# A graph-network kernel on one core: where two kinds of rounds put their type sums and their next first code sums

## The reference, cut to what matters

```python
h = relu(layernorm(x) @ node_proj_w.T + node_proj_b)
for l in range(2):
    trans = einsum('nh,tdh->tnd', h, edge_W[l])          # 8 matrices of 128 x 128
    agg = segment_sum(trans[edge_type, src], dst, 6250)  # 100,000 edges
    h = relu(gru_cell(agg, h, ...))                      # gates r, z, n
return x + h @ out_w.T + out_b
```

## Time and profile before

| What | us |
|---|---|
| Median of 3 runs | 2007.2 |
| Lowest and highest of the runs | 2001.24, 2015.2 |
| The profiled execution | 2021.61 |
| Its span in the profile | 2019.8 |
| Mean granted share of TensorE's clock | 0.886 |

### The profile page before, as it was taken

One profiled execution on the slowest core, in us unless ns is written; L12 is line 12 of the kernel. 1 busy time (PEld: TensorE's weight loads), 2 busy tenths in 40 slices (PEclk: granted clock), 3 DMA queues, 4 the chain that ended last, 5 costly groups with the idle time before them and its releaser, 6 DMA issues.

```text
span 2019.8 us, 32542 instructions
## 1 busy us (share of the span) xinstructions
PE 1548.0 (77%) x10440; PEld 1066.8 (53%) x10441; DVE 806.9 (40%) x3362; ACT 499.7 (25%) x959; POOL 1194.0 (59%) x1277
## 2 busy tenths in 40 slices
PE   6477888787878866877883888878787786687877
PEld 3244555454555544655662555545545454565665
DVE  6656262523433244454442223212433224444444
ACT  5233151513324112222220101110423411121222
POOL 6555666565666666666625666565565666666661
PEclk9688899998999978898885998899898997888889
DMA  8323728264462422222213866674334255222221
GB/s 196 110 63 103 238 84 270 59 218 128 148 205 64 137 73 79 78 79 77 77 36 105 273 226 225 219 254 129 85 105 117 77 140 116 73 73 72 70 75 30
DMA packets 183275, 251.81 MB, mean 125 GB/s; under 512 B 24322, under 2 KB 156580, under 8 KB 183140
## 3 DMA queue, kind: packets, MB, share of 16 engines
q0 software_dynamic: 58176, 119.22, 21.7%
q1 hardware_dynamic: 118644, 128.45, 20.3%
q10 hardware_dynamic: 6320, 2.41, 0.5%
HBM read 211.87 MB, written 38.12 MB: 124 GB/s over the span
## 4 chain that ended last, share of the span: by engine, by line
PE 35%; another core or an unknown queue 31%; issue 11%; DVE 11%; DMA 4%; ACT 3%; DVEq 3%; SPq 2%; ACTq 0%; PEldq 0%
PE ps L1185 10%; PE ps L1257 5%; PE ps L1122 5%; PE ps L1162 4%; PE ps L1236 4%; DMA blocks<-node_table 4%; PE ps L1249 3%; PE ps L1228 2%; DVE acc L1850 1%; DVE onehot L1772 1%; DVE acc L1870 1%; ACT counts L871 1%; DVE onehot L1807 1%; DVE work L1728 1%
## 5 line engine op out<-in xcount | busy, mean ns | idle before, releaser
L660 POOL DMA_INDIRECT gath<-node_table,srcT x1212 | 1159.5, 957 | 774.7 <-issue 303.2
L1185 PE MATMUL ps<-counts,blocks 128*128 128x504 f16 (+3 forms) x1764 | 421.1, 386 | 66.8 <-issue 33.4
L1870 DVE TENSOR_TENSOR acc<-ps,acc 128x16 f32 x864 | 150.7, 174 | 792.4 <-remote 311.8
L950 ACT COPY sums_sb<-ps 128x512 f32<-128x512 f32 x216 | 126.3, 587 | 870.3 <-remote 600.3
L1185 PEld LDWEIGHTS ps<-counts,blocks 128*128 128x128 bf16 x1764 | 171.5, 101 | 266.1 <-issue 81.2
L1162 PE MATMUL ps<-work 128*128 128x392 bf16 x983 | 219.3, 358 | 119.5 <-ACT counts L871 43.2
L1257 PE MATMUL ps<-sums_sb,wT 128*128 128x128 f32 x1728 | 243.6, 299 | 59.9 <-ACT sums_sb L950 46.6
L1257 PEld LDWEIGHTS ps<-sums_sb,wT 128*128 128x128 f32 x1728 | 230.6, 212 | 74.6 <-ACT sums_sb L950 51.4
L1249 PE MATMUL ps<-onehot,gath 128*128 128x128 bf16 x2592 | 200.5, 230 | 62.6 <-issue 36.2
L1249 PEld LDWEIGHTS ps<-onehot,gath 128*128 128x128 bf16 x2592 | 177.8, 104 | 108.9 <-issue 74.9
L871 ACT CAST counts<-ps 128x392 f16<-128x392 f32 x429 | 188.3, 498 | 117.8 <-PE ps L1162 70.2
(11 more groups left out here) (209 smaller groups left out, 831.6 us busy)
## 6 DMA issues: line engine op xcount, KB each, us to landing
blocks<-node_table SPq DMA_DIRECT2D x84, 672.0 KB
kept_counts<-counts SPq DMA_DIRECT2D x28, 882.0 KB
counts<-kept_counts SPq DMA_DIRECT2D x28, 882.0 KB
gath<-node_table,srcT POOLq DMA_INDIRECT x1212
node_table<-gath SPq DMA_DIRECT2D x12, 360.0 KB, 4.5
node_table<-work SPq DMA_DIRECT2D x12, 360.0 KB
counts<-in_x_dram SPq DMA_DIRECT2D x1, 2880.0 KB
out_dram<-counts SPq DMA_DIRECT2D x12, 240.0 KB
```

What stands on the lines that cost most here:

```text
L660: nc.gpsimd.indirect_dma_start(out=gath[:, b, j, :], out_offset=None, in_=tables[l], in_offset=bass.IndirectOffsetOnAxis(ap=index, axis=0) ...
L950: act.copy(n_sb[:, b // 2, b % 2 * BG:(b % 2 + 1) * BG, :], narrow_sums[b % 2]) \
L1185: last = nc.tensor.matmul(head_ps[:, 0:COLS[share]], blocks[:, j % 2, at, part * H:(part + 1) * H], counts[:, a, 0:COLS[share]], start=(i ...
L1870: nc.vector.tensor_tensor(win, narrow_ps[q][:, g * NARROW:(g + 1) * NARROW], win, ALU.add) \
```

## The change

**Narrow rounds, PE.** The first types move behind sums 3. With a head the order becomes sums 0, head, sums 1, head, sums 2, head, sums 3, first types, head, second types. Without a head: sums 0, sums 1, r and hn, sums 2, in, sums 3, first types, z, second types, turning.

**Narrow rounds, DVE.** The one-hots of a half come ahead of everything else in it and wait for `sums_ready` of their slot instead of following the adds. The hots of the head come next, all of them ahead of the adds (`FIRST_HOTS` is gone).

**Narrow rounds, ACT, without head.** After copy 2 only tanh; the sigmoid of z comes after copy 3, with the new state and its rows.

**Late rounds, PE.** Sums 0 of the next round run between types 2 and types 3 of this one. The first late round's sums 0 run ahead of the loop, and the last round begins with its sums 1.

```diff
-                        update(b, n, begin, tile, head)
+                        if head is not None:
+                            head_slot(l, head + b)
+                        elif b == 1:
+                            piece(act, begin, gate_r, l + 1, tile)
+                        elif b == 2:
+                            piece(act, begin, gate_n, l + 1, tile)
+                        elif b == 3:
+                            piece(act, begin, gate_z_state, l + 1, tile)
+                def gate_z_state(s, i):
+                    gate_z(s, i)
+                    state_rows(s, i)
...
                     narrow_sums_of(k, 2)
                     if head is None:
                         piece(pe, begin, gate_in, l + 1, tile)
+                    else:
+                        head_slot(l, head + 2)
+                    narrow_sums_of(k, 3)
                     narrow_types(k, 0)
                     if head is None:
                         piece(pe, begin, gate_z, l + 1, tile)
                     else:
-                        head_slot(l, head + 2)
-                    narrow_sums_of(k, 3)
-                    if head is not None:
                         head_slot(l, head + 3)
                     narrow_types(k, 1)
...
                 def one_round(k, n, places):
                     begin, tile = round_tile(pe, mybir.EngineType.PE, n)
-                    sum_by_code(k, places[0][0], 0, places[0][1])
                     sum_by_code(k, places[1][0], 1, places[1][1])
...
                     by_type(k, 2)
+                    sum_by_code(k + SLOTS, places[SLOTS][0], 0, places[SLOTS][1])
                     by_type(k, 3)
                     piece(pe, begin, to_rows, l + 1, tile)
...
                 def last_round(k, places, begin=None):
-                    sum_by_code(k, places[0][0], 0, places[0][1])
...
-                def add_narrow(k, g0, q, after_head, hots):
-                    if len(hots) <= FIRST_HOTS:
-                        for g in hots:
-                            make_hots(g)
-                        hots = []
+                def add_narrow(k, g0, q, after_head):
...
-                            for more in hots[g * len(hots) // (2 * BG):(g + 1) * len(hots) // (2 * BG)]:
-                                make_hots(more)
...
                     for q in range(2):
                         g0 = n * ROUND + 2 * q * BG
+                        for b in (2 * q, 2 * q + 1):
+                            dve.wait_ge(sem_l["sums_ready"], k + (b + 1 + SLOTS))
+                            (one_hots if last else narrow_hots)(n * ROUND + (ROUND + b * BG), b)
                         if head is None and q == 0:
                             piece(dve, begin, before_tanh, l + 1, tile)
-                        hots = MADE[l].get(head + 2 * q, []) if head is not None else []
-                        add_narrow(k, g0, q, added_until(l, head + 2 * q) if head is not None else 0, hots)
-                        for b in (2 * q, 2 * q + 1):
-                            (one_hots if last else narrow_hots)(n * ROUND + (ROUND + b * BG), b)
+                        for g in MADE[l].get(head + 2 * q, []) if head is not None else []:
+                            make_hots(g)
+                        add_narrow(k, g0, q, added_until(l, head + 2 * q) if head is not None else 0)
```

More of the change, by code:

```diff
@@ L951, in narrow_round, with update @@
                            .then_inc(es[l]["sums_copied"], 1)
-                        update(b, n, begin, tile, head)
-                def update(b, n, begin, tile, head=None):
-                    if head is not None:
-                        head_slot(l, head + b)
-                    elif b == 1:
+                        if head is not None:
[9 more added lines that the diff above has]
+                    state_rows(s, i)
+                def update(b, n, begin, tile):
+                    if b == 1:
                         piece(act, begin, gate_r, l + 1, tile)
@@ L1296, in first_places @@
                 def first_places(phase, turns=0):
-                    places = [(phase + b) % PLACES for b in range(SLOTS)]
+                    places = [(phase + b) % PLACES for b in range(SLOTS + 1)]
                     return [(turns + ((phase + b) // PLACES + 1) * (16 * BG), place) for b, place in enumerate(places)]
                 def later_places(n):
-                    return [(n * (16 * BG) + 16 * BG, b) for b in range(SLOTS)]
+                    return [((n + b // SLOTS) * (16 * BG) + 16 * BG, b % SLOTS) for b in range(SLOTS + 1)]
                 def one_round(k, n, places):
                     begin, tile = round_tile(pe, mybir.EngineType.PE, n)
-                    sum_by_code(k, places[0][0], 0, places[0][1])
                     sum_by_code(k, places[1][0], 1, places[1][1])
@@ L1389, in _ @@
                 begun = NARROW_END * SLOTS - HEAD_BATCHES[l]
+                landed, place = first_places(begun)[0]
+                sum_by_code(NARROW_END * SLOTS, landed, 0, place)
                 with pe.Fori(0, turns) as t:
@@ L1406, in _ @@
                         pe.sem_inc(pass_begun, 1)
+                        sum_by_code(p * BATCHES, 16 * BG, 0, 0)
                         with pe.Fori(0, ROUNDS - 1) as n:
```

1 line of the change is left out of this document (removed).

## The result

| | us |
|---|---|
| median of before, beside the change (4 runs, 2001.2 to 2016.8) | 2011.2 |
| median of after (4 runs, 2030.5 to 2045.3) | 2038.9 |
| ratio | 1.012, 95% interval 1.007 to 1.017 |
| the profiled executions, before and after | 2021.6 and 2030.5 |

What follows compares the result with a forecast made beforehand. No engine was full (PE 77% busy), so PE's waits, for held signals, copies and DVE's work, were taken as the bound. Gains 12 + 6 + 4 + 3 = 25 us from the 2007.2 median gave 1982 us, range 1950 to 2022.

Steps and rivals of the forecast that it cites:

- the late order holds the last types: Late rounds: longer gather trains delay signals of types 3 and `to_rows` by 4.7 us; 2032 us, chance 0.20.
- The late rounds: Twenty late rounds: sums 0 cover the copy of slot 3; bounds 15 gained, 23 lost; 3 us gain taken.
- only after this longer train: Late rounds, rival of chance 0.20: signals of types 3 and `to_rows` come after POOL's second batch, 4.7 us later.
- sums 0 may be held with the others: Late rounds, argument against the rival of chance 0.20: the signal of sums 0 may itself come only with the train's end.
- The rounds without a head: Six narrow rounds: second types wait less for the copy of slot 3; 2 us a round, 12 us gain.
- partly reappears ahead of: Rounds without a head: part of the 5.2 us wait before the second types returns ahead of `to_rows`.
- the bound "nothing": Rounds without a head: lower bound of the gain per round; the upper was 5.2 us, all of the wait.
- My 2 us: Rounds without a head: gain taken per round, the one-hots' 1.68 us and a little of the cover.
- The signs that I asked for: Rounds without a head: second types' wait from 31 to under 10 us, rounds 35 to 37 about 22, new wait for ACT.
- The rounds with a head and the hots: Narrow rounds: 6 us gain in 48 head rounds from less copy wait, 4 us from hots ahead of the adds.
- The wait of 7.14 us in round 12: Round 12, near 163 us: PE's wait for hots should go once DVE makes hots ahead of the adds.
- The rival of pacing: All rounds: POOL's gather trains set the time, so PE's order gains little; 2001 us, chance 0.30.

Runs made afterwards that it cites:

- late_only_b: Against the kernel before, only the late rounds' new order (sums 0 of the next round ahead of types 3), measured again on a chip that holds signals: 2065.1 us, 1.0088.
- headless_only: Against the kernel before, the narrow rounds' new order (PE, ACT, DVE) in only the six rounds without a head: 2038.1 us, 0.9995.
- late_delayed: Kernel before with PE's late order, but POOL's batch for the place of sums 0 waits for one sum more: 2044.0 us, 1.0015.
- head_only: Against the kernel before, the narrow rounds' new order in only the 48 rounds with a head: 2025.4 us, 0.9963.
- few_before: Kernel before with three of four gathers left out in rounds 39 to 47 of both layers: 1901.7 us, 0.9349.
- few_late: Late order alone, with three of four gathers left out in rounds 39 to 47 of both layers: 1909.1 us, 0.9374 of the kernel before.
- both_delayed: Whole change, with POOL's batch for the place of sums 0 held back until sums 1: 2035.1 us, 1.0008 of the kernel before.
- after_masked_b: Whole change with the tile's number masked with 127, measured again on a chip that holds signals: 2047.9 us, 1.0081 of the kernel before.
- dve_only_b: Against the kernel before, only DVE's new order in narrow rounds, measured again on a chip that holds signals: 2033.2 us, 0.9999.

## Why the prediction failed

**The sign** came out the other way: 1982 us was forecast, 25 less, and the medians say 28 more. The rival that ends on the other side, *the late order holds the last types*, was the right mechanism, with a chance of 0.20. Its time, 2032 us, came near by errors that partly cancel, as follows.

**The late rounds: the step that failed.** I priced the delay of types 3 and `to_rows` at nothing because the adds of types 3 were held for 3 us in round 41 anyway, so that 1.15 us would fit in. That takes the end of the hold as fixed. It is not: it hangs on where the train of gathers lies, and the moved sums put a train of eight over types 3. I had written this as the rival, with 4.7 us a round and a need of 9 of 20 rounds. Measured: the delay of the adds grows by 1.8 and 4.1 us in the mean of a layer (`late_only_b`, 4.0 and 6.1 against 2.2 and 1.9), 15 of 18 rounds have types 3 inside the long train, and the ten rounds cost 13 and 16 us more, some 1.5 us a round. The rival's words *only after this longer train* are too strong as well, since in 8 of the 15 rounds the adds start before its end. So the rival's price (4.7 us for each round that is hit) was over twice what it is (30 / 15 = 2.0), and its number, half of the rounds, was too low. The argument that I held against it, *sums 0 may be held with the others*, is true of only some rounds: the signal of sums 0 has to arrive while POOL is at the batch before, and in the round shown it did, at the boundary (1892.01, idle of 0.63 us).

Against the 3 us forecast as a gain, the late order alone costs 18 us (0.88% of 2046.0): 21 of the 53 us between forecast (25 less) and result (28 more).

**The rounds without a head: 12 us forecast, none found.** `headless_only` measures 0.9995, and the profiles of kernels with the old and the new order cannot be told apart: before, `late_only_b`, `late_delayed`, `head_only`, `few_before` and `few_late` take 74.6 and 78.7 us in the mean, after, `both_delayed`, `after_masked_b` and `headless_only` 76.7 and 77.9. My text named the reason, that the wait *partly reappears ahead of* `to_rows`. The wrong word is "partly". The wait of 5.2 us was parallel to a chain (gate z, sigmoid, four steps, relu) that is as long, so the bound "nothing" was right: the state of round 36 is ready at 765.47 before and at 765.31 after. My 2 us counted the one-hots' 1.68 as gained, and they only moved to the other side of that chain. The signs that I asked for came in part all the same: the second types' wait went from 15.8 us to none in layer 1 (in layer 2 it stayed at 13.5 of 15.4), and the new wait appeared at `to_rows`. A wait that vanishes is no proof of a gain; the length of the rounds is.

**The rounds with a head and the hots: about right.** 6 and 4 us were forecast. `head_only` gains 7.5 us by its ratio (within 0 to 15). By the same marks in the profiles, kernels with the new order (`head_only`, after, `both_delayed`, `after_masked_b`) against those with the old (before, `late_only_b`, `late_delayed`, `few_before`, `few_late`, `headless_only`) take 121.3 against 125.4 us to sums 1 of round 11 of layer 1, 601.7 against 600.2 from there to round 35, 47.9 against 44.8 in round 12 of layer 2, and 536.0 against 546.8 from round 13 to 35. So layer 1 gains nothing clear (the 4 us at the start lie inside the scatter of the old kernels, 120.1 to 129.6 there), and layer 2 gives 11 and loses 3. Why layer 2 alone, and what its round 12 loses, I have not tried. That the gain of hots is theirs is not shown either. The wait of 7.14 us in round 12 did go, as forecast, but in `dve_only_b` PE's waits for hots fell from 35.0 to 10.3 us over the kernel, and its time stayed (0.9999).

**The rival of pacing** (0.30) holds on the other chip: there POOL's gathers follow each other every 1.25 us through the late rounds, 16 x 1.25 = 20.0 us, and ten rounds of layer 2 take 200.1:

```profile
1478.85 0.95 POOL L660 DMA_INDIRECT gath<-node_table,srcT  x1 [0.30 <-issue]
1480.10 0.95 POOL L660 DMA_INDIRECT gath<-node_table,srcT  x1 [0.30 <-issue]
1481.35 0.94 POOL L660 DMA_INDIRECT gath<-node_table,srcT  x1 [0.30 <-issue]
```

```profile
PE ps L1249 <- DMA gath<-node_table,srcT: 54.6, 26, 11.9
PE ps L1228 <- DMA gath<-node_table,srcT: 48.7, 39, 2.1
```

Here PE waits for gathers, and nothing in either order is worth more than 0.32%. On the chips that hold, a late round takes 25 us with all gathers and 18 with a quarter of them; how much of this is held signals and how much the gathers' own time is not separated.

**What stays open.** The narrow order gains 14 us (0.67%) where 22 was forecast. With the late order's 18 that makes 4 us more than before, and the whole change was measured at 16 and 24 us more (1.0081 and 1.012 of 2040 and 2011). These 12 to 20 us lie at the edge of the intervals. `both_delayed` misses its product in the same direction (0.9933 x 1.0015 = 0.995, measured 1.0008), which speaks for halves that disturb each other; the runs do not settle it.

**What would be kept.** The narrow order alone is the one version that measured faster than both kernels: 0.9933 (0.9895 to 0.9971), and no slower on the chip without holds. Whether its six rounds without a head should go back to the old order (0.9963 without them) the intervals do not tell.

## To carry to other kernels

When a signal is seen late, find out what ends the delay before counting the delay as cover: here it hung on a train of gathers, and an edit that freed a buffer early laid a longer train over the signal. When work is put under a wait, ask which chain runs beside the wait; if that chain is as long, the wait moves and the round stays. And where an order on one engine is changed for the sake of another, test the halves apart and together: DVE's new order was worth nothing alone and 3% as the condition of PE's.

## What the runs showed of the hardware

The same kernel takes 1624 us on one chip and 2040 us on others; the profiles there have granted clocks of 0.95 and of 0.87 to 0.90. On the first chip DVE's adds start 0.2 us after PE's recorded end (the late order's types 3, table above), whatever POOL does. On the others PE's signals are held while gathers run, in the late rounds of these profiles by up to 8.95 us. In the round shown of `late_only_b` the last gather ends at 1896.71, the adds start at 1897.69 and POOL's next gather at 1898.68; in other rounds the hold ends sooner, as said with the table.

No hold is seen in the rows on signals of DVE and ACT. In the midst of such a train DVE ends a step at 1887.40 and ACT's relu, which waits for it, starts at 1887.44. In round 36 of before ACT's copy ends at 763.77, while POOL's gather of 763.41 runs, and PE starts at 763.82.

The release does not wait for all of the gathers' data: in the round shown the trace has 28 landing events of the last four gathers, 13 of them spread from 1894.36 to 1896.92 and 15 in a burst from 1898.21 to 1898.45, which is after the adds had started. In round 36 of before the burst comes from 763.32 to 763.70, after the copy's start at 763.18. The kernels with few gathers take away both POOL's work and the data's move, so they do not tell which of the two holds the signals. What makes one chip hold signals and another not, no run here tells.

The Trainium skill says in Perfetto Trace Analysis, DMA Instruction — SWDGE (GPSIMD), that the profiled end of a gather is the end of its descriptors and not of the data's move. The trace agrees: in the round shown the last gather's recorded end is 1896.71, and the burst of landing events begins at 1898.21. The same page's Tensor Engine Instruction lets PE's signal follow PSUM's acknowledgement; the first chip's 0.2 us agrees with this, the others' delays of up to 8.95 us do not, and no step in that section accounts for them.
